# Graph layer on one core: edge stretches of 19, statistics two tiles ahead, and a preparation cut into pieces

## The reference

```
xn = layernorm(x)
agg(v)[d] = sum over edges (s, d) of v[s] / deg[d]      # edges taken in both directions
h  = relu(xn @ W0_0 + b + agg(xn) @ W1_0 + b)
g  = h @ W0_1 + b + agg(h) @ W1_1 + b
x  = x + g + linear_attention(xn)
x  = x + mixture_of_experts(layernorm(x))               # 8 experts, the best 2 per node
```

## Time and profile before

| | |
|---|---|
| median of 3 runs | 2323.24 us (2322.51 to 2326.59) |
| the profiled execution's own time | 2325.6 us |
| its span, first to last instruction | 2324.1 us |
| mean granted TensorE clock | 0.963 |
| TensorE matmul busy | 2083.6 us, 90% |
| VectorE busy | 1578.9 us, 68% |
| ScalarE busy | 1196.7 us, 51% |
| GpSimd busy | 372.9 us, 16% |

### The profile page before, as it was taken

One profiled execution on the slowest core, in us unless ns is written; L12 is line 12 of the kernel. 1 busy time (PEld: TensorE's weight loads), 2 busy tenths in 40 slices (PEclk: granted clock), 3 DMA queues, 4 the chain that ended last, 5 costly groups with the idle time before them and its releaser, 6 DMA issues.

```text
span 2324.1 us, 52608 instructions
## 1 busy us (share of the span) xinstructions
PE 2083.6 (90%) x15454; PEld 1319.6 (57%) x15455; DVE 1578.9 (68%) x4935; ACT 1196.7 (51%) x2466; POOL 372.9 (16%) x440
## 2 busy tenths in 40 slices
PE   2766778999999999999689999999999996899996
PEld 1655566565555555555344544444444443799996
DVE  6888877799999999999555453545544555355554
ACT  2555555355555555555365562444444443566664
POOL 2000000000000000000011110121122112366665
PEclk9898899899999999999899999999999998899998
DMA  2222223622222222222343335555555554665552
GB/s 78 78 67 70 74 74 102 193 117 117 112 114 118 112 116 115 111 112 115 118 152 127 124 120 202 207 193 188 204 198 190 195 206 138 175 97 93 89 92 46
DMA packets 158449, 299.19 MB, mean 129 GB/s; under 512 B 31614, under 2 KB 107695, under 8 KB 156131
## 3 DMA queue, kind: packets, MB, share of 16 engines
q1 hardware_dynamic: 130787, 243.71, 30.4%
q0 software_dynamic: 25856, 47.15, 9.2%
q10 hardware_dynamic: 1664, 6.35, 0.8%
HBM read 148.37 MB, written 144.19 MB: 126 GB/s over the span
## 4 chain that ended last, share of the span: by engine, by line
PE 74%; issue 9%; DVE 6%; ACT 2%; POOLq 2%; DVEq 2%; DMA 2%; POOL 1%; ACTq 1%; SPq 0%
PE bank L2231 45%; PE bank L2222 6%; PE bank L2447 6%; PE bank L2432 6%; POOLq L832 2%; PE bank L2100 2%; PE bank L2414 1%; PE bank L2064 1%; PE bank L2074 1%; PE bank L2239 1%; PE bank L2379 1%; DVEq L1099 1%; ACT big L1782 1%; DMA big<-rows_dram 1%; PE bank L2085 1%
## 5 line engine op out<-in xcount | busy, mean ns | idle before, releaser
L2231 PE MATMUL bank<-RW,big 128*128 128x512 f16 x4802 | 1159.6, 380 | 4.9 <-DMA big<-a_dram 4.7
L2231 PEld LDWEIGHTS bank<-RW,big 128*128 128x128 f16 x4802 | 436.3, 98 | 395.8 <-issue 9.1
L1880 ACT ACTIVATE big<-bank 128x512 f16<-128x512 f32 (+1 forms) x640 | 364.1, 573 | 316.1 <-PE bank L2222 314.7
L1258 DVE TENSOR_TENSOR big<-iotaB,keys 128x512 f16<-128x512 f16 x1300 | 451.7, 416 | 7.9 <-issue 6.6
L2222 PEld LDWEIGHTS bank<-big 128*128 128x128 f16 x2560 | 191.0, 98 | 105.8 <-issue 1.4
L2222 PE MATMUL bank<-big 128*128 128x128 f16 x2560 | 247.5, 219 | 0.1
L964 POOL DMA_INDIRECT out_dram<-big x112 | 180.8, 1614 | 111.7 <-ACT big L2025 77.1
L900 POOL DMA_DIRECT2D big<-in_L_ffn_W_dram x8 | 6.4, 802 | 1117.2 <-DVE R L1317 1115.6
L2016 ACT ACTIVATE big<-bank,b1A,iscA 128x256 f32<-128x256 f32 x224 | 114.3, 560 | 100.4 <-PE bank L2432 95.1
L2447 PE MATMUL bank<-RW,big 128*128 (+1 forms) x1344 | 157.7, 274 | 0.0
L2432 PE MATMUL bank<-big,RW 128*128 128x256 f16 x1344 | 157.0, 274 | 0.4 <-ACT big L2005 0.4
(11 more groups left out here) (420 smaller groups left out, 2942.9 us busy)
## 6 DMA issues: line engine op xcount, KB each, us to landing
big<-a_dram SPq DMA_DIRECT2D x49, 800.0 KB, 6.0
big<-a_dram SPq DMA_DIRECT2D x49, 768.0 KB, 4.5
a_dram<-big SPq DMA_DIRECT2D x49, 640.0 KB, 3.0
a_dram<-big SPq DMA_DIRECT2D x49, 512.0 KB, 2.6
a_dram<-big SPq DMA_DIRECT2D x49, 416.0 KB, 2.4
big<-rows_dram SPq DMA_DIRECT2D x56, 265.0 KB
big<-in_x_dram SPq DMA_DIRECT2D x96, 128.0 KB, 2.1
own_dram<-big SPq DMA_DIRECT2D x48, 256.0 KB, 2.5
```

The source lines that it names most:

```text
L1258: last = v.tensor_tensor(out[q].rearrange("p b (m k) -> p b m k", k=2), inturn(iotaB[:, :], QB, P // 2), twice(kd[:, q * QB:(q + 1) * QB, ...
L1880: a.activation(Ab[q][:, 0:n], banks[BB(q)][:, 0:n], ACT.Copy).then_inc(s_ab, 1)
L2231: last = mm(bank[:, :], blk(q, c), R2[:, u * 2 * D:(u + 1) * 2 * D], start=(i == 0), stop=(i == T - 1))
```

## The change

- CAP becomes 19: windows of 128 x 19 edges, and all per-edge work with 19 columns.
- `prepare` is cut into `words1`, `keys1`, `same1` and `within1`; for group g they run behind tiles 2, 3, 4 and 5 of the group before, in place of one block behind tile 3.
- The comparison of keys reads overlapping ranges. The keys of a tile lie in `keyw` behind 19 cells of -1, and one instruction compares each key with the AHEAD = 18 cells ahead of it. The mask and its product are gone; two additions and a reduction, which now runs across rows of 19, remain.
- Statistics run ahead: two sets of them and three `xin` buffers. `inverse(t+1)` stands behind `ranks(t)`, `deviation1(t+2)` in ScalarE's tile t, and `normal1(t)` ahead of `base1(t+1)`.

```diff
-CAP = 20
+CAP = 19
+AHEAD = CAP - CAP % 2
...
-        key1 = wr.f16(T * CAP)
+        keyw = wr.f16(PACK * 2 * CAP).rearrange("p (t c) -> p t c", c=2 * CAP)
...
-        same = wr.f16(PACK * CAP * CAP)
-        ahead = wr.f16(PACK * CAP * CAP)
+        same = wr.f16(PACK * AHEAD * CAP).rearrange("p (t d c) -> p t d c", t=PACK, c=CAP)
...
-        offs = sb("offs", [P, 1])
-        rstd = sb("rstd", [P, 1])
+        offs = sb("offs", [P, 2])
+        rstd = sb("rstd", [P, 2])
...
-        xin = [sp1.f32(D) for _ in range(2)]
+        xin = [sp1.f32(D) for _ in range(3)]
...
-            sp.dma_start(xin[0], io["x"][0:P, :]).then_inc(s_x[0], 16)
-            sp.dma_start(xin[1], io["x"][P:2 * P, :]).then_inc(s_x[1], 16)
+            for t in range(3):
+                sp.dma_start(xin[t], io["x"][t * P:(t + 1) * P, :]).then_inc(s_x[t], 16)
...
-                if t + 2 < T:
+                if t + 3 < T:
                     sp.wait_ge(s_xn, t + 1)
-                    if t + 2 < T - 1:
-                        sp.dma_start(xin[t % 2], io["x"][(t + 2) * P:(t + 3) * P, :]).then_inc(s_x[t % 2], 16)
+                    if t + 3 < T - 1:
+                        sp.dma_start(xin[t % 3], io["x"][(t + 3) * P:(t + 4) * P, :]).then_inc(s_x[t % 3], 16)
                     else:
-                        sp.dma_start(xin[t % 2][LAST:P, :], zeros32[LAST:P, 0:D]).then_inc(s_xz, 16)
+                        sp.dma_start(xin[t % 3][LAST:P, :], zeros32[LAST:P, 0:D]).then_inc(s_xz, 16)
                         sp.wait_ge(s_xz, 16)
-                        sp.dma_start(xin[t % 2][0:LAST, :], io["x"][(T - 1) * P:N, :]).then_inc(s_x[t % 2], 16)
+                        sp.dma_start(xin[t % 3][0:LAST, :], io["x"][(T - 1) * P:N, :]).then_inc(s_x[t % 3], 16)
...
-            def prepare(g):
+            def tile(ap):
+                return ap.rearrange("p (t c) -> p t c", c=CAP)
+            def words1(g):
...
-                def tile(ap):
-                    return ap.rearrange("p (t c) -> p t c", c=CAP)
+            def keys1(g):
+                sl = slice(g * NK, (g + 1) * NK)
...
-                v.tensor_tensor(key1[:, sl], tF, movF, ALU.add)
+                v.tensor_tensor(keyw[:, :, CAP:2 * CAP], tile(tF), tile(movF), ALU.add)
                 v.tensor_tensor(key2[:, sl, :], deep(tF, [P, NK, 2]), deep(movF, [P, NK, 2]), ALU.add)
                 dve.drain()
-                for i in range(PACK):
-                    ks = slice(g * NK + i * CAP, g * NK + (i + 1) * CAP)
-                    v.tensor_tensor(same[:, i * CAP * CAP:(i + 1) * CAP * CAP].rearrange("p (a m k) -> p a m k", a=CAP, k=2),
-                                    inturn(key1[:, ks], CAP, CAP // 2), twice(key2[:, ks, :], CAP, CAP // 2), ALU.is_equal)
-                dve.drain()
-                v.tensor_tensor(ahead.rearrange("p (i n) -> p i n", i=PACK),
-                                same.rearrange("p (i n) -> p i n", i=PACK),
-                                wide(earlier[:, :], [P, PACK, CAP * CAP]), ALU.mult)
-                dve.drain()
-                av = ahead.rearrange("p (c n) -> p c n", n=CAP)
-                sv = same[:, 0:NK * CAP // 2].rearrange("p (c n) -> p c n", n=CAP // 2)
-                v.tensor_tensor(sv, av[:, :, 0:CAP // 2], av[:, :, CAP // 2:CAP], ALU.add)
-                dve.drain()
-                v.tensor_tensor(sv[:, :, 0:4], sv[:, :, 0:4], sv[:, :, 6:10], ALU.add)
-                dve.drain()
-                v.tensor_reduce(within[:, sl], sv[:, :, 0:6], AX.X, ALU.add)
+            def same1(g):
+                first = keyw[:, :, CAP - AHEAD:2 * CAP]
+                pitch, _ = first.ap[0]
+                before = bass.AP(first.tensor, first.offset, [[pitch, P], [2 * CAP, PACK], [1, AHEAD], [1, CAP]])
+                v.tensor_tensor(same, before,
+                                keyw[:, :, CAP:2 * CAP].rearrange("p t (a c) -> p t a c", a=1)
+                                .to_broadcast([P, PACK, AHEAD, CAP]), ALU.is_equal)
+                dve.drain()
+            def within1(g):
+                n = AHEAD
+                while n > 5:
+                    h = n - n // 2
+                    v.tensor_tensor(same[:, :, 0:n - h, :], same[:, :, 0:n - h, :], same[:, :, h:n, :], ALU.add)
+                    dve.drain()
+                    n = h
+                v.tensor_reduce(tile(within[:, g * NK:(g + 1) * NK]),
+                                same[:, :, 0:n, :].rearrange("p t d c -> p t c d"), AX.X, ALU.add)
...
+                i = t % 2
                 dve.wait_ge(s_std, t + 1)
-                if t:
-                    dve.wait_ge(s_xn, t)
-                v.reciprocal(rstd[:, :], sums[:, 3:4])
-                dve.drain()
-                v.tensor_tensor(offs[:, :], sums[:, 1:2], rstd[:, :], ALU.mult).then_inc(s_stat, 1)
+                if t >= 2:
+                    dve.wait_ge(s_xn, t - 1)
+                v.reciprocal(rstd[:, i:i + 1], sums[:, i, 3:4])
+                dve.drain()
+                v.tensor_tensor(offs[:, i:i + 1], sums[:, i, 1:2], rstd[:, i:i + 1], ALU.mult).then_inc(s_stat, 1)
...
-            prepare(0)
+            v.memset(keyw, -1.0)
+            inverse(0)
+            words1(0)
+            keys1(0)
+            same1(0)
+            within1(0)
             onehots(0, 0)
             for t in range(T):
-                inverse(t)
+                g, i = t // PACK + 1, t % PACK
                 if t + 1 < T:
                     onehots(t + 1, (t + 1) % 2)
                 ranks(t, t % 2)
-                if t % PACK == PACK // 2 and t // PACK + 1 < NG:
-                    prepare(t // PACK + 1)
+                if t + 1 < T:
+                    inverse(t + 1)
+                if g < NG:
+                    if i == 2:
+                        words1(g)
+                    if i == 3:
+                        keys1(g)
+                    if i == 4:
+                        same1(g)
+                    if i == 5:
+                        within1(g)
...
-                act.wait_ge(s_x[t % 2], 16 * (t // 2) + 16)
-                if t:
-                    act.wait_ge(s_stat, t)
+                s4 = sums[:, t % 2, :]
+                act.wait_ge(s_x[t % 3], 16 * (t // 3) + 16)
+                if t >= 2:
+                    act.wait_ge(s_stat, t - 1)
                 act.drain()
-                a.activation(xsq, xin[t % 2], ACT.Identity, accum_out=sums[:, 0:1])
+                a.activation(xsq, xin[t % 3], ACT.Identity, accum_out=s4[:, 0:1])
                 act.drain()
-                a.activation(sums[:, 1:2], sums[:, 0:1], ACT.Copy, scale=-1.0 / D)
+                a.activation(s4[:, 1:2], s4[:, 0:1], ACT.Copy, scale=-1.0 / D)
                 act.drain()
-                a.activation(xsq, xin[t % 2], ACT.Square, bias=sums[:, 1:2], accum_out=sums[:, 2:3])
+                a.activation(xsq, xin[t % 3], ACT.Square, bias=s4[:, 1:2], accum_out=s4[:, 2:3])
                 act.drain()
-                a.activation(sums[:, 3:4], sums[:, 2:3], ACT.Sqrt, scale=1.0 / D, bias=epsc[:, :]).then_inc(s_std, 1)
+                a.activation(s4[:, 3:4], s4[:, 2:3], ACT.Sqrt, scale=1.0 / D, bias=epsc[:, :]).then_inc(s_std, 1)
...
-                a.activation(xs[:, 0:D], xin[t % 2], ACT.Identity, scale=rstd[:, :], bias=offs[:, :]).then_inc(s_xn, 1)
+                i = t % 2
+                a.activation(xs[:, 0:D], xin[t % 3], ACT.Identity, scale=rstd[:, i:i + 1], bias=offs[:, i:i + 1])\
+                 .then_inc(s_xn, 1)
                 act.drain()
-            def parts1(t):
+                a.activation(R2[:, bass.ds(t * 2 * D, D)], xs[:, 0:D], ACT.Copy, scale=S).then_inc(s_xhi, 1)
+            def low1(t):
+                a.activation(R2[:, bass.ds(t * 2 * D + D, D)], banks[5][:, D:2 * D], ACT.Copy, scale=S).then_inc(s_xlo, 1)
+            deviation1(0)
+            deviation1(1)
+            base1(0)
+            for t in range(T):
                 normal1(t)
-                a.activation(R2[:, bass.ds(t * 2 * D, D)], xs[:, 0:D], ACT.Copy, scale=S).then_inc(s_xhi, 1)
-                if t >= 3:
-                    own1(t - 3)
-                if t + 1 < T:
-                    deviation1(t + 1)
-                place1(t)
-                a.activation(R2[:, bass.ds(t * 2 * D + D, D)], banks[5][:, D:2 * D], ACT.Copy, scale=S).then_inc(s_xlo, 1)
-            base1(0)
-            deviation1(0)
-            for t in range(T):
...
-                parts1(t)
+                if t >= 3:
+                    own1(t - 3)
+                if t + 2 < T:
+                    deviation1(t + 2)
+                place1(t)
+                low1(t)
```

More of the change, by code:

```diff
@@ L145, in gps_layer @@
         lastc = sb("lastc", [P, 2, T], F16)
-        earlier = sb("earlier", [P, CAP * CAP], F16)
         flip = sb("flip", [P, P], F16)
@@ L184, in gps_layer @@
         rd2 = sb("rd2", [P, T])
-        sums = sb("sums", [P, 4])
+        sums = sb("sums", [P, 2, 4])
         iota8 = sb("iota8", [P, 8])
@@ L414, in gps_layer @@
```

(6 more changed lines are left out.)

## The result

| | before | after |
|---|---|---|
| median of the runs of one chip (lowest to highest) | 2324.31 us (2322.51 to 2326.59), 4 runs | 2259.86 us (2255.62 to 2266.12), 4 runs |
| the profiled execution, its span | 2325.6 us, 2324.1 us | 2261.03 us, 2259.5 us |
| VectorE's decode behind the stage starts | 397.98 us | 333.03 us |
| from there to the span's end | 1926.1 us | 1926.5 us |

The ratio is 0.9724, 95% interval 0.9699 to 0.975: 64 us less, where 61 were forecast (2262 from 2323.2). All of it is in the stage: the decode starts 64.95 us earlier, and what follows takes 0.4 us longer.

The account below looks back on a forecast made before the run. VectorE was taken as busiest, held up by a ring through ScalarE's square root. Terms of 68 us, less 5 for clock and 1 for window 13, gave 2261, plus 1 for the reduction: 2262 us (own range 2254 to 2272).

Parts of the forecast that it names:

- waits for the root: VectorE's reciprocal waits in 34 pieces for ScalarE's square root; statistics two tiles ahead remove them, 37.2 us.
- 19 columns: VectorE's per-edge products and reductions get shorter with fewer columns, 166 ns a tile, 8.1 us over 49 tiles.
- key ranges: Overlapping compare without mask saves 2.7 us in each of 7 preparations, 18.9 us; 1 us put aside for its reduction.
- start: At the stage's start, first statistics and inverse(0) are hidden inside VectorE's wait for the windows: 0.3 us gained.
- end: At the stage's end, VectorE's 5.24 us wait before the decode shrinks to 1.8: 3.5 us gained.
- window 13: Group 1's windows are needed one tile earlier, this one arriving just when words1(1) asks: zero to 1 us lost.
- clock: Kept back for drops of TensorE's granted clock in the stage that outrun the slack: 5 us.
- The rival that the roots stay late: ScalarE's own order keeps the square roots late, so 33.4 us of waits stay: 2295 us, chance 0.05.
- The rival of 2277: VectorE's two-byte preparation work with odd starts runs at one element per cycle, 14.7 us given back; chance 0.15.
- the rival of 2286: TensorE's half-clock tiles with a piece outrun the slack, 4 us in each of six groups, 24 us; chance 0.20.
- The slower rival: TensorE never returns to 2.4 GHz in the stage, each tile costs 8.8 us: 2398 us, chance 0.04.
- TensorE is only a fraction behind: At the stage's end, gram and own largely run beside the last ranks, leaving a wait of 1.8 us.

Follow-up runs that it names:

- experiment 1: Kernel before with the statistics two tiles ahead and nothing else (third xin buffer and ScalarE's order included): 2283.47 us, ratio 0.9828.
- experiment 4: Changed kernel with 20 columns (CAP = 20): 2269.59 us, ratio 0.9766.
- experiment 11: Changed kernel with 18 columns (CAP = 18), all edges of this case still in the windows: 2249.86 us, ratio 0.9692.
- Experiment 3: Changed kernel with the four preparation pieces as one block behind tile 3 of the group: 2257.43 us, ratio 0.9715.
- experiment 8: Changed kernel with TensorE's 19 count matmuls of each tile issued twice: 2261.5 us, ratio 0.973.
- experiment 7: Kernel before with TensorE's 20 count matmuls of each tile issued twice: 2348.09 us, ratio 1.0102.
- Experiment 10: Changed kernel with the second load of the last x tile moved behind the two stores on SP's queue: 2255.24 us, ratio 0.9702.
- experiment 5: Kernel before with one small addition of ranks more per tile on VectorE: 2327.74 us, ratio 1.0013.

## Why the prediction was right

The stage lost 64.95 us. By the prediction's own terms:

| term | forecast | measured | from |
|---|---|---|---|
| waits for the root | 37.2 | 40.3 | 37.2 + 34 x 0.09; experiment 1 has 40.9 |
| 19 columns | 8.1 | 8.3 | 49 x (4.94 - 4.77) |
| key ranges | 18.9, less 1 | 15.4 | 6 x (9.93 - 7.70) + first one 10.14 - 8.13 |
| start | 0.3 | 1.1 | first preparation at 27.02 for 28.14 |
| end | 3.5 | 1.5 | wait 3.73 for 5.24 |
| window 13 | -1 | -1.3 | the wait of L1047 |
| clock | -5 | 0 | no wait of VectorE on ScalarE's base |
| sum | 61 | 65.3 | |

**Statistics.** Right, and shown from both sides: the lead alone brings 41 us, its removal costs 28. The rival that the roots stay late is out. What was missed is the 0.09 us of each wait.

**Columns.** Right to 0.2 us; experiments 4 and 11 give the same size in both directions.

**Key ranges.** The mechanism was right, the sizes were somewhat off. The compare took 1.47 us for 1.41, the first addition 0.79 for 0.78, the second 0.45 for 0.42: the rate of the rows it was taken from, not half of it. Between the two additions, each with an operand that starts at an odd element, (789 - 446) / (1197 - 532) = 0.52 ns per element; between those of experiment 4, with even starts, (881 - 525) / 700 = 0.51. The rival of 2277 is out. Here the Trainium skill had differed with itself. The trace agrees with the Trainium skill's "Vector Engine (DVE) Microarchitecture Reference", section 5.1, and not with the 4-byte start of "Advanced Engine Details and Errata", 2x-1p Requirements.

The mis-sized term is the reduction, sized at 0.85 us and measured at 1.33: (1329 - 155) / 665 = 1.77 ns per element across rows of 19, against 1.04 along rows. It is the step and not the short sum: the old L1088 sums 6 elements a time along the row, at 1.04, and the new one 5. The trace of experiment 4 gives (1386 - 1329) / 35 = 1.6 for the added elements. "Vector Engine (DVE) Microarchitecture Reference", section 5.2 of the Trainium skill, has 1.73 to 2.51 ns per column where a source hops at every element; it measured this on 4-byte words and two sources. The trace, with two-byte elements and one source, lies at the low end of that. Over seven preparations the difference is 3.4 us, of which the prediction had put aside 1; its upper end for it was 4.9. The row that the 0.85 came from was a contiguous one, so it could only be a lower end. The term also makes up nearly all of the gap between the 7.2 us forecast for a preparation's parts and the 7.70 measured.

**Pieces.** That they only move work was right. Experiment 3 adds that they aren't needed: TensorE's idle stretches of a block (waits of 7.9 us at most there) are covered by the slack. In the change TensorE waits at most 2.8 us behind a piece, near the 2.5 forecast, but for the one case below.

**TensorE's clock.** The step that kept back 5 us, and the rival of 2286, failed at one point: they took every tile with a piece as cold from end to end. The clock does still fall. Its deepest fall comes with TensorE's longest wait inside the stage, 4.98 us, where 21 small instructions that run once in the stage stand behind a piece (first two rows). Around the pieces from 180 to 206 us it doesn't fall at all (third row):

```profile
224.00:228.00 4.00, 0.00 (x0) 0.00 (x0) 3.06 (x22) 0.00 (x0) 0.00 (x0) 0.64 0.46 138
228.00:232.00 4.00, 3.73 (x29) 3.18 (x30) 3.61 (x7) 2.40 (x9) 0.00 (x0) 0.51 0.00 0
...
164.00:224.00 60.00, 48.43 (x573) 40.17 (x571) 54.02 (x127) 44.66 (x148) 0.00 (x0) 1.00 0.32 93
```

The slack takes up what does fall: experiments 3 and 8, with a lower clock and with more of TensorE's work, don't lengthen the stage. The slower rival needed 60% of the tiles cold; the mean granted clock was 0.94. TensorE's own tile was also sized too long, at 4.66 and 4.6 us. The 0.69 us of L2064 in that sum is a duration; the next work starts 0.52 us after it (experiment 7), and the tile measures 4.40 (experiment 8). So VectorE was the longer by 0.37 us and not 0.2. A small misreading, on which nothing hangs: the row has TensorE at 8 tenths in slice 7, not 6 to 7.

**Start.** The first words come at 27.02 us here, but at 25.37 in the trace of experiment 8, with the same start; with the old start they come at 28.14, 27.57 and 27.25. What ends VectorE's wait is now the statistics (8.1 us), not the windows, which are there earlier than forecast. Why, wasn't tried.

**End.** The step "TensorE is only a fraction behind" failed: it was late by the 2.33 us it waited for ScalarE, which waited for a store. Experiment 10 gives 1.6 of the missing 2.0 us. The groups of the kernel before had that wait too, and it wasn't read:

```profile
L1763 ACT ACTIVATE big<-bank 128x512 f32<-128x512 f32 x42 | 24.4, 581 | 2.5 <-DMA own_dram<-big 2.5
```

The 5.24 us that the term started from was also a matter of that one trace. Experiments 5 and 7 leave the old kernel's end as it is and have 2.18 and 2.45 us there. From 390 to 398 us the granted clock was 0.66 in the trace of the kernel before (first row) and 1.00 in that of experiment 5 (second row):

```profile
390.00:398.00 8.00, 6.91 (x53) 5.74 (x51) 2.46 (x6) 2.52 (x8) 0.00 (x0) 0.66 0.29 98
...
390.00:398.00 8.00, 5.82 (x45) 5.04 (x46) 4.06 (x9) 5.01 (x15) 0.00 (x0) 1.00 0.17 57
```

So the term's 3.5, and the 1.5 of the table, hold for this pair of traces; against the end of experiments 5 and 7 the change's 3.73 is a loss of 1.3 to 1.6.

So the nearness of 61 to 65 is in part luck: 5 us kept back for nothing stand against 3.1 not seen in the waits, while the key ranges had 2.5 too much and the end 2.0.

**What stays open.** From the decode to the span's end the profiled executions of the twelve experiments take 1922 to 1931 us with the same code, and four executions of the change differ by 10.5 us in all. VectorE's wait for `fit` behind the stage varies too, from 3.4 to 6.4 us, but not with it: 3.4 at 1922.0, 6.3 at 1924.0, 3.4 at 1926.5. What sets either wasn't tried. Differences under 5 us between medians are therefore read here by stage time alone.

## What to carry to other kernels

Where an engine's waits are many, short and of one kind, draw the ring that they close: one more tile of lead in a two-instruction step removed 41 us, more than either shortening of the work. An engine that works 4.88 us a tile beside one of 4.77 isn't the bound when the other has extra work in every group and there is a lead between them. Before spending effort on an engine, lengthen it by a known amount: 0.27 us of VectorE cost 5 us before and 13 after, 0.5 us of TensorE 22 before and nothing after, which tells the bound better than the busy shares. And price an instruction by a row with the same stride, not only the same size.

## What the runs showed of the hardware

- Two-byte additions with an operand at an odd start and rows of 19 run at the rate of those at even starts and rows of 20: 0.52 and 0.51 ns per element, between two additions of one trace each.
- A reduction that steps 19 elements costs 1.77 ns per element, one along the row 1.04 (both by the same fixed 155 ns); contiguous additions in its place took 0.33 us less per preparation.
- A recorded wait of VectorE costs about 0.09 us more than its length, for without one the next instruction starts 0.08 us before the last one's end (0.91 us after a start of 0.99 us).
- More work on an engine that idles need not cost its full length in busy time: 23.5 us of TensorE's matmuls added 12.1 us, at a mean granted clock of 0.95 for 0.94.
